# An AdaLN attention and expert-routing block: one attention turn, two small preparations and two late rank computations change places

## What is computed

```python
h = _layernorm(x) * (1 + ca) + sa
att = softmax(einsum('blhd,bmhd->blmh', q, k) * scale, axis=2)
opt = einsum('blmh,blhd->blhd', att, v)
x = x + ga * (opt @ w_out.T + b_out)
h = _layernorm(x) * (1 + cb) + sb
x = x + gb * (probs[argmax] * expert[argmax](h))
```

## Time and profile before

| | us |
|---|---|
| median of 3 runs | 639.82 |
| lowest, highest | 638.85, 641.99 |
| the profiled execution | 639.67 |
| its span | 637.9 |

### The profile page before, as it was taken

How to read it: one execution, slowest core, us unless ns; L and a number is a source line. 1 busy time by engine, 2 the same in 40 slices (tenths; PEclk the granted TensorE clock), 3 DMA queues, 4 the chain that set the end, 5 groups by cost and what they waited for, 6 DMA issues and landing times.

```text
span 637.9 us, 11675 instructions
## 1 busy us (share of the span) xinstructions
PE 468.4 (73%) x2517; PEld 268.8 (42%) x2517; DVE 547.6 (86%) x1336; ACT 539.9 (85%) x2306; POOL 476.9 (75%) x663
## 2 busy tenths in 40 slices
PE   5457688787778778778778877878766439998880
PEld 2113334343344334334334433433333338887770
DVE  6988999999999999999999999999988537866670
ACT  1599999999999999999999999999999127766650
POOL 4456666888888888888888888888877626777774
PEclk9555655655665655665665565565555559999995
DMA  6355554445554545455455554544441165667640
GB/s 190 108 152 149 155 155 140 142 144 148 150 143 139 152 140 169 135 156 150 140 154 154 149 145 137 154 126 118 132 141 57 46 197 169 190 190 195 197 132 4
DMA packets 75346, 91.64 MB, mean 144 GB/s; under 512 B 12841, under 2 KB 58959, under 8 KB 75275
## 3 DMA queue, kind: packets, MB, share of 16 engines
q1 hardware_dynamic: 66742, 72.93, 41.7%
q0 software_dynamic: 6560, 16.83, 7.0%
q10 hardware_dynamic: 1976, 1.15, 0.7%
HBM read 58.41 MB, written 33.29 MB: 144 GB/s over the span
## 4 chain that ended last, share of the span: by engine, by line
ACT 64%; PE 8%; DMA 7%; POOL 7%; DVE 5%; issue 5%; SPq 2%; POOLq 0%; ACTq 0%; DVEq 0%
ACT scores L714 63%; DMA out_dram<-out_room,x_s 3%; DMA x_s<-table 3%; POOL out_dram L692 3%; PE scores L986 2%; PE scores L995 2%; DVE neg_max L1093 1%; SPq L455 1%; POOL rstd L581 1%; PE side_a L864 1%; PE scores L978 1%; DMA x_s<-in_x_dram 1%; DVE bn L1018 1%; POOL table L642 0%; DMA parts_dram<-parts 0%
## 5 line engine op out<-in xcount | busy, mean ns | idle before, releaser
L714 ACT ACTIVATE scores<-scores,neg_max 128x256 f32<-128x256 f32 x1024 | 467.8, 870 | 12.4 <-DVE neg_max L1093 12.3
L714 ACT ACTIVATION_READ_ACCUMULATOR scores<-scores,neg_max 128x1 f32 x1024 | 440.6, 631 | 0.0
L1093 DVE TENSOR_REDUCE neg_max<-scores 128x4 f32<-128x1024 f32 x256 | 309.7, 1212 | 6.9 <-PE scores L836 6.4
L836 PE MATMUL scores<-k_stack,q_stack 64*128 64x256 bf16 x1024 | 148.6, 389 | 90.5 <-ACT scores L714 78.6
L836 PEld LDWEIGHTS scores<-k_stack,q_stack 64*128 64x128 bf16 x1024 | 34.0, 106 | 172.0 <-ACT scores L714 140.9
L692 POOL DMA_INDIRECT out_dram<-out_room,x_s x77 | 78.5, 1020 | 36.9 <-DVE out_room L1497 19.5
L642 POOL DMA_INDIRECT table<-rows,place_i x64 | 65.8, 1028 | 18.9 <-issue 18.9
L783 ACT ACTIVATE hid<-scores,w_e 128x128 f32<-128x128 f32 x154 | 48.2, 364 | 18.4 <-PE scores L986 18.1
L864 PE MATMUL side_a<-w_gated,opt_t 128*128 128x128 f32 x128 | 50.9, 502 | 0.0
L986 PE MATMUL scores<-x_t,w_e 128*128 128x128 f32 x308 | 49.4, 284 | 1.7 <-ACT x_t L776 1.7
L580 POOL TENSOR_TENSOR rstd<-mv,eps_s 128x4 f32<-128x4 f32 x37 | 7.4, 199 | 57.8 <-DVE mv L1049 42.9
(11 more groups left out here) (148 smaller groups left out, 848.3 us busy)
## 6 DMA issues: line engine op xcount, KB each, us to landing
x_s<-table SPq DMA_DIRECT2D x77, 192.5 KB, 2.7
q_stack<-parts_dram SPq DMA_DIRECT2D x192, 64.0 KB, 2.6
parts_dram<-parts SPq DMA_DIRECT2D x31, 384.0 KB, 2.7
k_stack<-parts_dram SPq DMA_DIRECT2D x186, 64.0 KB, 2.2
mod_b<-mod_rows SPq DMA_DIRECT2D x32, 256.0 KB, 3.5
x_s<-in_x_dram SPq DMA_DIRECT2D x13, 256.0 KB, 3.1
w1x_s<-in_w1x_dram SPq DMA_DIRECT2D x7, 258.0 KB, 2.9
w_s<-in_w_dram SPq DMA_DIRECT2D x7, 256.0 KB, 3.0
```

Source lines behind the costliest of these rows:

```text
L714: last = act.activation(buf[:, k * L:k * L + L], buf[:, k * L:k * L + L], ACT.Exp, bias=neg_max[:, p, n:n + 1], accum_out=exp_sum[:, p, n: ...
L836: last = pe.matmul(scores[:, c, at:at + L], q_stack[p][r, g + j, t * P:t * P + P], k_stack[p][r, g + j, :], start=True, stop=True)
L1093: dve.tensor_reduce(to, scores[:, (PAIRS * b.n + i) % RING, :].rearrange("p (e j m) -> p e j m", e=2, j=2), AX_X, ALU.max, negate=True).th ...
```

## The change

On PE, unit 5 of each batch is made ahead of turn_att instead of behind it, and in batches 30 and 31 (whole) rank stands behind unit 2 instead of ahead of project_out. On DVE, in those batches, the steps that use the ranks stand behind the maximum of unit 3 instead of ahead of it. prepare_map goes from batch 3 (ahead of unit 3) to batch 1 (ahead of unit 7), and gated_bias_low from batch 0 (ahead of unit 7) to batch 1 (behind unit 3). On SP, the store of the bias parts goes from batch 0 to batch 1, and with it the wait for that store and the load of bias_rows; all three stand there ahead of store_parts. No instruction is added or taken away.

```diff
--- before.py
+++ after.py
@@ -523,17 +523,18 @@
                 if b.n == 0:
                     sp.wait_ge(mod_ready, 1)
                     sp.dma_start(mod_rows, rows_out[:, :, :].rearrange("b r d -> b (r d)")).then_inc(mod_stored, 16)
+                else:
+                    load_mod(b)
+                if b.n == 1:
                     sp.wait_ge(bias_ready, 1)
                     sp.dma_start(bias_dram.rearrange("r (b d) -> b r d", d=D), bias_out[:, :, :]).then_inc(bias_stored, 16)
-                else:
-                    load_mod(b)
+                    sp.wait_ge(bias_stored, 16)
+                    sp.dma_start(bias_rows[:, :, :].rearrange("r b d -> r (b d)"), bias_dram).then_inc(bias_loaded, 16)
                 if b.ago(-2).there():
                     store_parts(b.ago(-2))
                 if b.n == 0:
                     sp.wait_ge(mod_stored, 16)
                     load_mod(b)
-                    sp.wait_ge(bias_stored, 16)
-                    sp.dma_start(bias_rows[:, :, :].rearrange("r b d -> r (b d)"), bias_dram).then_inc(bias_loaded, 16)
                 if b.ago(-2).there():
                     sp.wait_ge(scored, PAIRS * b.n + PAIRS)
                     load_stacks_by(sp, b.slot(2), (0, 1))
@@ -919,11 +920,11 @@
                 if placing(b):
                     rank(placing(b), b.n - 2)
                 score(b, 1)
-                if whole(b):
-                    rank(whole(b), b.n - 2)
                 if b.ago(2).there():
                     project_out(b.ago(2))
                 score(b, 2)
+                if whole(b):
+                    rank(whole(b), b.n - 2)
                 if b.ago(-2).there():
                     turn_x(b.ago(-2))
                 score(b, 3)
@@ -931,9 +932,9 @@
                 if b.ago(-2).there():
                     project_q(b.ago(-2))
                     project_k(b.ago(-2))
+                score(b, 5)
                 if b.ago(1).there():
                     turn_att(b.ago(1))
-                score(b, 5)
                 score(b, 6)
                 if b.ago(2).there():
                     turn_h2(b.ago(2))
@@ -1338,14 +1339,14 @@
                     make_h(ahead)
                 if b.n == 0:
                     modulate(1)
-                if b.n == 3:
-                    prepare_map()
+                row_max(b, 3)
+                if b.n == 1:
+                    gated_bias_low()
                 if routed:
                     find_place(routed)
                     count_rows(routed)
                     own_place(routed)
                     note_place(routed)
-                row_max(b, 3)
                 if marked:
                     highest(marked)
                     compare(marked)
@@ -1380,8 +1381,8 @@
                     take_h2(norm)
                 if marked:
                     mark(marked)
-                if b.n == 0:
-                    gated_bias_low()
+                if b.n == 1:
+                    prepare_map()
                 row_max(b, 7)
                 if tail.there():
                     weigh_values(tail)
```

## The result

| | before | after |
|---|---|---|
| median, us (20 runs each) | 640.39 | 642.05 |
| the profiled execution | 639.67 | 643.68 |
| its span | 637.9 | 641.9 |

The ratio is 1.0027, with an interval from 1.0018 to 1.0037: the change costs 1.2 to 2.4 us where 1.0 was to be won.

A forecast was written before the change was run, and what follows sets the result against it. The prediction took ACT's exponentials, counted by distances of starts, to bound the kernel until the drain. Its terms, 4.2 - 1.07 - 2.3 - 1.3 - 0.5 = -1.0 us, took 639.67 to 638.7, range 636.2 to 641.8.

The forecast's parts named there:

- The side within 0.5%: Whole kernel: measured time within 0.5% of before, chance 0.82; faster by more had 0.12, slower by more 0.06.
- bias parts: Batch 2, unit 2: project_out waits for bias_rows until 56.3, so ACT loses 4.2 us, between 2.7 and 5.8.
- prepare_map: Batch 3, unit 3: ACT on time once its six DVE instructions leave, 1.07 us gained; zero cost in batch 1.
- unit 5: Unit 5 ahead of turn_att: 0.19 us gained in each of 12 odd batches, 2.3 in all, bounds 0 and 4.1.
- late ranks: Batches 30 and 31: project_out no longer held behind rank, 1.3 us gained, between 0.6 and 1.7.
- drain: End of attention: POOL's root starts earlier because the means come earlier, 0.5 us gained, between 0 and 1.
- The estimate of a loss of 1.7 us by the fixed cost alone: Bias load: at about 2.0 us per DMA without a queue, bias_rows is there at 53.8, losing 1.7 us.
- Two side predictions: SP, batch 3: parts store takes about 2.8 us instead of 5.5; stacks issued at 57.4 instead of 55.74, delay hidden.
- The give-back of 0.2 per batch at unit 4: Batches 30 and 31: rank steps and weights between the maxima of units 3 and 4 cost 0.2 us per batch.
- Rival 1: Order of unit 5 gains nothing because DVE's work ends last: 641.0, up to 642.6 with bias at its upper bound; chance 0.2.
- Rival 2: Even batches gain too, 0.15 us at unit 5 and 0.04 at unit 3: 2.3 more, 636.4; chance 0.14.
- a dear bias load: Batch 2, unit 2: the bias load costs 5.8 us, its upper bound, giving 640.3; chance 0.06 as a rival.

The follow-up runs named there:

- turn_only: Kernel before with only unit 5 put ahead of turn_att in every batch: 641.03 against 641.43 us, ratio 0.9994.
- fill4: Kernel before with four spare bn_stats on DVE ahead of the maxima of unit 5 in 12 odd batches, 7 to 29: 642.00 us, ratio 1.0015.
- fill2: Kernel before with two spare bn_stats on DVE ahead of the maxima of unit 5 in 12 odd batches, 7 to 29: 641.07 against 640.76 us, ratio 0.9998.
- bias_only: Kernel before with only the bias parts made, stored and loaded in batch 1: 645.24 against 641.43 us, ratio 1.0053.
- pad_later: Changed kernel with SP's late pieces of empty table rows issued one batch later: 640.19 us against 640.76 for before, ratio 0.9986.
- rank_only: Kernel before with only rank and the steps using it moved later in batches 30 and 31: 640.27 against 641.43 us, ratio 0.9979.
- early_pad: early plus the late pieces of empty table rows at the ends of batches 1 to 3: 667.16 us where before takes 670.5, ratio 0.9955.
- early_all: early_pad with prepare_map in batch 10 ahead of unit 7: 670.16 us where before takes 670.5, ratio 0.9992.
- early_pad_again: Same program as early_pad, timed again on another chip: 638.24 us against 640.82 for before, ratio 0.9956.
- map_only: Kernel before with only prepare_map moved to batch 1 ahead of unit 7: 641.28 against 641.43 us, ratio 0.9997.
- bias_back: Changed kernel with the bias parts put back to batch 0: 639.09 us against 640.76 for before, ratio 0.9971.
- early: Changed kernel, bias parts in batch 0, gated_bias_low behind unit 7's maxima, batch 1's x statistics behind unit 0's: 669.33 us where before takes 670.5, ratio 0.9985.

## Why the prediction was wrong

It gave 638.7 in a range of 636.2 to 641.8; 642.05 lies 0.25 above the range. Of the 3.35 us of error 0.7 is the base: the forecast started from the profiled execution, 639.67, and the median of before is 640.39. The other 2.7 is in the steps. The side within 0.5% came true, the sign of the change did not. Step by step, against the profile after:

| step | predicted | in the trace of after | alone, measured |
|---|---|---|---|
| bias parts | +4.2 | +3.88 (end of unit 2's first; its start +4.12) | +3.4 (2.6 to 4.2) |
| prepare_map | -1.07 | -0.59 | -0.2 (-1.0 to +0.6) |
| unit 5 | -2.3 | 0 | -0.4 (-0.9 to +0.2) |
| late ranks | -1.3 | -0.97 | -1.3 (-2.0 to -0.7) with the drain |
| drain | -0.5 | -0.63 | |
| sum | -1.0 | +1.7 | +1.5; the whole +1.7 |

The spans of the two profiles differ by 4.0. What the table doesn't hold is ACT's pace, 1.0 us over the attention part, and some 1.3 us behind the drain, where nothing was changed.

**The step that failed** is in the first paragraph of the prediction: "The idle column of the waits is not a good measure of that. [...] I use the distances of starts instead." The first half was right that a late start is partly hidden in the durations. The conclusion was the wrong way round: what is hidden there is not lost. turn_only shows it (0.19 less late twelve times, 2.3 by starts, 0.4 measured and at most 0.9), fill4 shows the other side (0.31 later twelve times, 3.7 by starts, 1.0 measured), and fill2, with a smaller dose, agrees. All three terms that the sum took too high come from this one reading. Unit 5: 12 x 0.19 = 2.3 where the ends show 0. prepare_map: 1.07 by starts; by ends 73.48 + 0.45 less 71.96 + 0.93 is 1.04, less 0.45 is 0.59. The late ranks: 1.11 at unit 2 by starts; by ends 467.41 + 0.45 less 465.85 + 0.97, less 0.45, is 0.59, with 0.38 more at three other units. The idle column had 0.47 at both places, nearer to the ends' 0.59 than 1.07 was. 2.3 + 0.48 + 0.33 = 3.1, less 0.13 in the drain and 0.32 in the bias parts, is the 2.7 us between -1.0 and +1.7. The number that the prediction had in hand and explained away was the pace, 29.26: it read 0.52 of loss into it because it took 0.449, the pace of starts while the lag grows, for the price of an exponential.

**Bias parts.** Right in mechanism, and in size within the interval of the run alone, link by link: issued at 49.30 (49.8 predicted), landed 53.9 (54.1), bias_rows at 56.1 (56.3), ACT's unit 2 at 60.39 (60.45). The store took longer than I gave it, 4.6 instead of 4.3, but left earlier; in bias_only it left at 50.14 and took 4.4. "Nothing later gives it back" was probably too strong, by what unit 0 of batch 5 shows under bias_only. The rule of the Trainium skill that the prediction weighed ("DMA: Bandwidth & Descriptors", "Queues, rings and completion order") is borne out as far as the runs go: the same store took 2.9 us in batch 0, 3.7 in pad_later, 4.4 in bias_only and 4.6 here, longer with more issued ahead of it by SP. Whether it is the order of a ring or a mere sharing of the DMA engines the runs don't tell. The estimate of a loss of 1.7 us by the fixed cost alone, which the prediction took from the section "Anatomy of one DMA" of the same page of the Trainium skill, was wrong; that section gives the figure for DMAs which POOL issues, and this store is SP's. Two side predictions held: the parts store took 2.8 us behind the stall (54.27 to the stacks at 57.10), and the stacks' delay was hidden.

"What batch 0 gains is nothing" was right as well: DVE merely waits for the x load. DVE of after at the x load, and then the copy of prepare_map in batch 1:

```profile
35.95 0.49 DVE L1019 BATCH_NORM_STATS2 bn<-x_s 128x6 f32<-128x128 f32 x2 [1.99 <-DMA x_s<-in_x_dram]
...
47.72 1.10 DVE L1304 COPY sums_of<-expert_s 77x14 f32<-77x14 f32 x1
```

The 0.79 us at unit 7 are gone from ACT, but unit 0 of batch 1 again starts 1.67 us after the load has landed (35.92, then 37.59). It starts 0.7 earlier than in before because SP came to that load 1.4 us earlier (31.09 against 32.49), ahead of every instruction that the change touches. The same scatter of the start, not the change, is the likeliest reason why the bias store left 0.5 us sooner than forecast.

**prepare_map.** "In batch 1 it costs 1.1 to 2.3 us of DVE" was right (47.25 to 49.43 is 2.2), and so was "at worst 0.7 late": 0.54 by starts, 0.37 by ends. In after this goes under in the stall that follows, since that stall is set by SP, and the 0.59 of batch 3 stays won. Alone, without the stall, it costs what it wins.

**Late ranks and drain.** Right, with 0.33 less of the ranks than forecast and 0.13 more of the drain. The residual on DVE has no wait for PE in batch 30. POOL of after in the drain:

```profile
496.56 0.96 POOL L643 DMA_INDIRECT table<-rows,place_i  x1 [0.30 <-issue]
497.55 0.21 POOL L581 TENSOR_TENSOR rstd<-mv,eps_s 128x4 f32<-128x4 f32 x1
```

POOL's root came 2.7 us later than in before (494.86) while ACT's last exponential ended 3.3 later (496.68 against 493.36): 0.6 won. The test that the prediction named, the root "no longer right behind a scatter", was wrong, though: it still is, since the scatter moved with it. The give-back of 0.2 per batch at unit 4 did not come.

**The rivals.** Rival 1, unit 5 gains nothing, came true with 0.2 of the chance and gave 641.0; with 0.8 us added by the two other steps mis-sized the same way it is 641.8, less 0.3 and 0.1 for the bias parts and the drain 641.4. But its condition was not the one it named (DVE free for under 0.05 us): DVE did get free, and ACT did start on time. Rival 2 was the same error once more. The range missed because it treated the steps as separate, while one mistake in the measure sat in three of them. It also did not hold what it said: "rivals 1 and 2 with their ends" reaches to rival 1's own upper end of 642.6, and the range stopped at 641.8. That 642.05 lies under 642.6 would have been luck, since that end stood for a dear bias load, and the bias load was not dear.

## What to carry to other kernels

Before you count lateness of a busy engine, take start plus duration for a few neighbouring instructions: if the ends stay evenly spaced while starts jump and durations shrink by as much, the engine is full, and the jumps are an echo of its own lag. A stretch whose pace equals count times the distance of ends has nothing to give to a change of order. At most such a change makes the lag longer, and the lag then covers a late start further on, as the 0.4 us of batch 30 in turn_only. A tiny store with a wait and a load behind it belongs where the queue is short and two batches pass before anyone needs it; here moving it one batch later turned slack into 4 us of stall, which ate all that the sound parts won.

## What the runs showed of the hardware that was not expected

- **The lag of ACT.** An exponential of 256 columns with its sum: 0.449 us from start to start while it runs ahead, 0.455 from end to end, recorded durations from 0.45 up to 1.34 (mean 1002 ns in after), with no standstill at either. turn_only and after show the larger durations and are no faster for it at this place.
- **ACT has two paces.** In profiled executions an even batch took 14.56 or 14.57 us by its ends in before, rank_only, bias_only, fill4, early_pad, early_all and early_pad_again, and 14.59 or 14.60 in after, turn_only, map_only, bias_back, pad_later, fill2 and early. That is some 1.0 us over the kernel, not tied to any edit that I can name (early and early_pad differ only in the padding), and a part of the 3.3 us by which after's profiled attention part ended later. The profiled executions at the slower pace lie on average 1.0 us above the median of their own program, the others 0.3 below it, which speaks for a trait of the execution and not of the program. Its cause is open.
- **The x load ahead of batch 1** made ACT stand 0.44 us in before, 0.71 in after, 1.85 in bias_only and not at all in turn_only, with the same DMA in the same place of SP's list. SP came to it between 31.1 and 33.1 us, and it took 4.2 to 4.8 us to land. In all nine programs without the edits of early in which DVE waited for it, ACT's unit 0 of batch 1 starts 1.67 us after the landing. k_stack ahead of batch 5 scatters as much: ACT stood there for 0 in before and 1.59 in fill2, whose edit begins in batch 7. A single profile can't price an edit near either to better than a microsecond.
- **DVE held while POOL works.** The same instruction, L1281, took 0.27 us in the row of early_pad_again above and 1.12 in before, where it starts with a long step of POOL already running; so did the copy into sums_of, 1.10 us, beside POOL's L447. DVE, then POOL, of before:

```profile
32.99 1.12 DVE L1281 TENSOR_TENSOR bias_out<-bias_f 32x128 bf16<-32x128 f32 x1
```

```profile
32.82 1.15 POOL L444 TENSOR_TENSOR rest<-qk,parts 128x512 f32<-128x512 f32 x1
```

  The Trainium skill ("SBUF — State Buffer", "SBUF: two separate sides") has an exclusive lock on a port pair that the two engines share, held for a whole instruction. The rows agree: DVE's ends 0.14 us after POOL's.
- **One chip took 29 us more for the experts** than the others, in every kernel run there, with an unchanged attention part. Only ratios within one chip were used.
